# Two DRAM copies of the convolution's kernel rows, one for each half of the partitions

## What is computed

```python
def _L0_cond_ref(u, length, ...):          # B, H, L = 32, 64, 1024
    u_m = u * mask[:, None, :]
    kernel = _get_kernel(log_dt, C, log_A_real, A_imag, Lq)      # H x L
    y = irfft(rfft(u_m, n=2*Lq) * rfft(kernel, n=2*Lq))[..., :Lq]
    y = y + u_m * D[:, None]
    return y * mask[:, None, :]

def _L0_ffn_ref(x, ...):                   # hidden 1024, inner 2752
    gate, up = x2 @ Wg, x2 @ Wu            # weights unpacked from 4 bits
    return (gate * sigmoid(gate) * up) @ Wd

x = x + _L0_ffn_ref(_L0_cond_ref(x, ...))
```

## Time and profile before

| | us |
|---|---|
| median of 3 runs | 1163.69 (1163.19 to 1167.55) |
| profiled execution, its own time | 1166.86 |
| its span, first to last instruction | 1164.7 |
| mean granted TensorE clock | 0.993 |
| TensorE busy | 1141.1 (98%) |
| VectorE / ScalarE / GpSimd busy | 889.0 / 845.4 / 221.9 |
| 64 Toeplitz loads, issue to landing | 3.6 / 6.5 / 14.4 (min / median / max) |
| 9 kernel-row stores, issue to landing | 2.0 / 3.4 / 5.4 |

### The profile page before, as it was taken

How to read it: one execution, slowest core, us unless ns; L and a number is a source line. 1 busy time by engine, 2 the same in 40 slices (tenths; PEclk the granted TensorE clock), 3 DMA queues, 4 the chain that set the end, 5 groups by cost and what they waited for, 6 DMA issues and landing times.

```text
span 1164.7 us, 14987 instructions
## 1 busy us (share of the span) xinstructions
PE 1141.1 (98%) x5490; PEld 949.0 (81%) x5490; DVE 889.0 (76%) x987; ACT 845.4 (73%) x1402; POOL 221.9 (19%) x139
## 2 busy tenths in 40 slices
PE   5999999999999999999999999999999999999996
PEld 5999998788888888888888888888888888888884
DVE  7668746677777777777777887788788777777777
ACT  6443214888788788788788797887888788788773
POOL 0121000211422432121121251211211211211113
PEclk7999999999999999999999999999999999999999
DMA  7778779441553566434433874456655434434515
GB/s 275 274 230 254 251 246 255 113 109 27 151 149 100 135 161 166 121 87 109 117 100 101 237 210 125 106 154 193 160 154 141 122 101 117 109 88 121 129 39 212
DMA packets 76191, 176.03 MB, mean 151 GB/s; under 512 B 20870, under 2 KB 26438, under 8 KB 76118
## 3 DMA queue, kind: packets, MB, share of 16 engines
q1 hardware_dynamic: 74050, 173.24, 52.6%
q10 hardware_dynamic: 2036, 1.81, 0.5%
q0 software_dynamic: 32, 0.03, 0.0%
HBM read 159.94 MB, written 15.83 MB: 151 GB/s over the span
## 4 chain that ended last, share of the span: by engine, by line
PE 95%; DMA 1%; DVE 1%; issue 1%; POOL 0%; ACT 0%; DVEq 0%; POOLq 0%; SPq 0%
PE pair L1266 28%; PE pair L1307 27%; PE pair L1287 27%; PE pair L1219 12%; DMA toep<-kernel_padded 1%; POOL o L592 0%; DMA kernel_padded<-k_sb 0%; PE pair L1199 0%; PE pair L1177 0%; DMA logs<-in_L_cond_log_dt_dram 0%; DVE q_in L1061 0%; ACT size L644 0%; DVEq L165 0%; DVE exps L794 0%; ACT L646 0%
## 5 line engine op out<-in xcount | busy, mean ns | idle before, releaser
L1036 DVE SCALAR_TENSOR_TENSOR acc<-pair,s_down,acc 128x1024 f32<-128x1024 f32 x328 | 420.3, 1283 | 185.3 <-PE pair L1307 183.8
L711 ACT ACTIVATE pair<-pair,ratio 128x512 f32<-128x512 f32 x616 | 381.7, 664 | 99.5 <-PE pair L1266 99.2
L730 ACT ACTIVATE pair<-pair,ratio 128x512 f32<-128x512 f32 x581 | 360.2, 658 | 114.1 <-PE pair L1287 113.9
L1266 PE MATMUL pair<-high,wg 128*128 128x512 f32 x704 | 278.4, 395 | 0.0
L1266 PE MATMUL pair<-low,wg 128*128 128x512 f32 x704 | 276.1, 392 | 0.0
L1307 PE MATMUL pair<-mid_h,wd 128*128 128x512 f32 x688 | 268.7, 392 | 0.0
L1287 PE MATMUL pair<-high,wu 128*128 128x512 f32 x672 | 265.7, 395 | 0.0
L1307 PE MATMUL pair<-mid_l,wd 128*128 128x512 f32 x672 | 264.4, 393 | 0.0
L1287 PE MATMUL pair<-low,wu 128*128 128x512 f32 x672 | 263.4, 392 | 0.0
L544 POOL CAST mid_h<-sil 128x1024 fp32r<-128x1024 f32 (+1 forms) x43 | 45.3, 1052 | 688.3 <-DVE sil L1013 677.8
L1266 PEld LDWEIGHTS pair<-high,wg 128*128 128x128 f32 x704 | 132.1, 188 | 33.0 <-ACT pair L711 1.1
(11 more groups left out here) (154 smaller groups left out, 577.8 us busy)
## 6 DMA issues: line engine op xcount, KB each, us to landing
q_in<-rows_backwards SPq DMA_DIRECT2D x86, 512.0 KB, 4.7
z_in<-zeros_plus_one SPq DMA_DIRECT2D x130, 256.0 KB, 4.6
toep<-kernel_padded SPq DMA_DIRECT2D x64, 512.0 KB, 6.5
q_in<-_L_ffn_down_qweight_dram SPq DMA_DIRECT2D x42, 512.0 KB, 4.6
u_all<-in_x_dram SPq DMA_DIRECT2D x13, 512.0 KB, 10.7
x_fin<-in_x_dram SPq DMA_DIRECT2D x12, 512.0 KB, 9.0
out_dram<-x_fin SPq DMA_DIRECT2D x12, 512.0 KB, 5.2
high_parts<-staged SPq DMA_DIRECT2D x8, 512.0 KB, 3.0
```

The lines of the kernel that those rows point to most:

```text
L711: act.activation(gate_ps[:, tb, :], gate_ps[:, tb, :], ACT.Copy, scale=ratio[:, 0, G * t + g:G * t + g + 1]).then_inc(gate_scaled, 1)
L730: act.activation(up_ps(tau)[:, tb, :], up_ps(tau)[:, tb, :], ACT.Copy, scale=ratio[:, 1, G * t + g:G * t + g + 1]).then_inc(up_scaled, 1)
L1036: dve.scalar_tensor_tensor(out=acc[:, hid, :], in0=ps, scalar=scale, in1=acc[:, hid, :], op0=ALU.mult, op1=ALU.add).then_inc(down_taken, 1)
L1266: mm = pe.matmul(gate_ps[:, tb, :], w["g"][tau % 2][:, g, :], rows[:, g, 512 * tb:512 * tb + 512], start=g == 0 and part == 0, stop=part = ...
```

## The change

`kernel_padded` gets a second copy of all 64 rows. Every store of a chunk becomes two stores of the same `k_sb`, one to each copy; the zeros are written to both. Every Toeplitz load becomes two loads: partitions 0 to 63 read from copy 0, partitions 64 to 127 from copy 1, each 64 windows of 4 KB. The semaphores count 32 instead of 16 for a load, for a store and for the zeros.

```diff
--- before.py
+++ after.py
@@ -158,7 +158,7 @@
 
 def build_program(nc, x, itok, log_dt, C, log_A, A_imag, D, gq, gs, gz, uq, us, uz, dq, ds, dz,
                   ctab, stab, ident_in, out):
-    kpad = nc.dram_tensor("kernel_padded", (H, KPAD), F32, kind="Internal").ap()
+    kpad = nc.dram_tensor("kernel_padded", (2, H, KPAD), F32, kind="Internal").ap()
     rows_back = nc.dram_tensor("rows_backwards", (2 * TAIL + 1, 16, G, P), I32, kind="Internal").ap()
     high_back = nc.dram_tensor("high_parts", (KT, P, HALF), F32, kind="Internal").ap()
     zscr = nc.dram_tensor("zeros_plus_one", (3, ROWS, P), BF16, kind="Internal").ap()
@@ -361,23 +361,26 @@
             sp.dma_start(lens_i[:], bass.AP(itok.tensor, 0, [[0, P], [1, B]])).then_inc(lens_in, 16)
             for g in range(6, 14):
                 sp.dma_start(x_in(g), x_rows(g)).then_inc(x_loaded[g], 16)
-            sp.wait_ge(zero_stored, 16)
+            sp.wait_ge(zero_stored, 32)
 
             def store_kernels(c):
 
                 h0, n = CHUNKS[c]
                 sp.wait_ge(k_sb_ready, c + 1)
-                dst = bass.AP(kpad.tensor, h0 * KPAD, [[32, 32], [KPAD, n], [1, 32]])
-                sp.dma_start(dst, k_sb[:, 0:n, :]).then_inc(k_stored, 16)
-                sp.wait_ge(k_stored, 16 * (c + 1))
+                for copy in range(2):
+                    dst = bass.AP(kpad.tensor, (copy * H + h0) * KPAD, [[32, 32], [KPAD, n], [1, 32]])
+                    sp.dma_start(dst, k_sb[:, 0:n, :]).then_inc(k_stored, 16)
+                sp.wait_ge(k_stored, 32 * (c + 1))
 
             def load_toeplitz(g):
                 for hh in range(HG):
                     slot = HG * (g % 2) + hh
                     if g >= 2:
                         sp.wait_ge(conv_mm, (g - 2) * HG + hh + 1)
-                    src = bass.AP(kpad.tensor, (g * HG + hh) * KPAD, [[1, P], [1, L]])
-                    sp.dma_start(toep[:, slot, :], src).then_inc(t_loaded[slot], 16)
+                    for copy in range(2):
+                        p0 = P // 2 * copy
+                        src = bass.AP(kpad.tensor, (copy * H + g * HG + hh) * KPAD + p0, [[1, P // 2], [1, L]])
+                        sp.dma_start(toep[p0:p0 + P // 2, slot, :], src).then_inc(t_loaded[slot], 16)
 
             store_kernels(0)
             load_toeplitz(0)
@@ -521,7 +524,8 @@
             pool.memset(s_rows[:], 1.0).then_inc(rows_clear, 1)
             pool.memset(z_rows[:], 0).then_inc(rows_clear, 1)
             pool.wait_ge(const_ready, 1)
-            pool.dma_start(kpad[:, L:KPAD], zero[:]).then_inc(zero_stored, 16)
+            for copy in range(2):
+                pool.dma_start(kpad[copy, :, L:KPAD], zero[:]).then_inc(zero_stored, 16)
 
             pool.wait_ge(ai_loaded, 16)
             pool.wait_ge(c_loaded, 16)
@@ -914,7 +918,7 @@
                 h0, n = CHUNKS[c]
                 dve.wait_ge(k_mm, c + 1)
                 if c > 0:
-                    dve.wait_ge(k_stored, c * 16)
+                    dve.wait_ge(k_stored, c * 32)
                 do(dve.tensor_copy(k_sb[:, 0:n], k_ps[0:32, 0:32 * n].rearrange("p (h b) -> p h b", h=n)))
                 d_piece = bass.AP(d_row[:].tensor, h0, [[H, 32], [1, n], [1, 1]])
                 dve.tensor_tensor(k_sb[:, 0:n, 31:32], k_sb[:, 0:n, 31:32], d_piece, ALU.add).then_inc(k_sb_ready, 1)
@@ -1209,7 +1213,7 @@
                         multiply_kernel(chunk_begun_at(g - 2))
                     n = HG * g + hh
                     slot, k = n % TRING, hh // 2
-                    pe.wait_ge(t_loaded[slot], 16 * (n // TRING + 1))
+                    pe.wait_ge(t_loaded[slot], 32 * (n // TRING + 1))
                     if hh == 0:
                         pe.wait_ge(u_all_ready, 2 * HEAD_TURNS if g == 1 else 2 * g + 2)
                     if hh % 2 == 0 and g >= 2:
```

## The result

The changed kernel takes 1204.09 us in the median of 4 runs (1203.32 to 1210.85), the kernel before 1165.48 beside it: 1.034 times, 95% interval 1.032 to 1.037, 38.6 us slower. The forecast was 1181, 17 us slower. The measured time lies inside the range, 1170 to 1214, but where the rival "in between" (1190 to 1205) put it. The mechanism forecast is there, and it is less than half of the matter.

The account below looks back on a forecast made before the run. The prediction took TensorE, busy 98% of the span, to bound the kernel. Late loads at group 10 (13.3 us), at group 15 (1.7) and slower half loads (2.1) added 17.1 to 1163.7, giving 1181 us; range 1170 to 1214.

Parts of the forecast that it names:

- in between: Toeplitz loads: halves run at 205 to 250 GB/s, the DMA queue bounds now and then, 1190 to 1205 us; chance 0.16.
- The mechanism forecast: SP queue: added issues and second stores make Toeplitz loads late, so TensorE stalls; 13.3 us at group 10, 1.7 at group 15.
- Does half a load cost half?: SP queue: no; each added load issue costs 0.47 us, with 0.36 as the lower end.
- the 15.0 of the sum: SP queue, groups 2 to 9: added issues for 32 heads at 0.47 us each, 15.0 us.
- The queue's waits for others soak up 2.1: SP queue up to group 10's loads: its waits for others absorb 2.1 us, leaving those loads 15.6 us late.
- Rate of the half loads: DMA queue: half loads move at 250 GB/s, showing only behind the first weight loads, 2.1 us more for group 15's first head.
- The prediction's own sign: DMA, 60 to 120 us: share near 0.8 with 250 GB/s or more, or above 0.85 with about 200 or less for half rate.
- the halves also transfer at half rate: Toeplitz loads: halves go one behind the other, a head at about 205 GB/s; +50 us, 1213 us; chance 0.27.
- Not slower: Toeplitz loads: a second copy relieves a DRAM hot spot, giving back 6.6 us of store landings; 1166 us; chance 0.12.

Follow-up runs that it names:

- e2: The changed kernel with whole loads instead of cut ones, even heads from copy 0 and odd heads from copy 1, two stores per chunk: 1167.6 us.
- e7: The kernel before with its 64 weight transfers issued by ScalarE's queue instead of SP's: 1167.9 us.
- e9: Against the kernel before: two copies, one whole load per head, even partitions reading copy 0 and odd partitions copy 1: 1168.8 us.
- e4: The kernel before, one copy, with each head's load cut into even and odd partitions: 1180.8 us.
- e1: The kernel before, one copy and one store per chunk, with each head's load cut at partition 64: 1202.8 us.
- e5: The changed kernel with its 64 weight transfers issued by ScalarE's queue instead of SP's: 1193.5 us.
- e8: The kernel before, one copy, with partitions 0 to 63 loaded from SP's queue and 64 to 127 from GpSimd's: 1196.5 us.
- e10: The kernel before, one copy, with each head's load cut into three: partitions 32 to 95, 0 to 31 and 96 to 127: 1210.2 us.
- e3: The kernel before, one copy, with each head's load cut into two column halves over all 128 partitions: 1173.3 us.

## Why the prediction was wrong

**What bounds the kernel, what the change may win.** Right. The bound is TensorE; the convolution's losses go through nearly one for one (span +37.4, feed-forward stage +40.2 late and 2.8 shorter); nothing was to be won, which e2, e7 and e9 confirm from three sides.

**"Does half a load cost half? ... I take 0.47 us for each added issue."** The step that failed first. The direction was right and the row that told the truth was cited: L413, 64 partitions, at 636 ns against L417's 552. I used it only to exclude a cheaper half load and took the price of a whole one. Measured: 0.596 us an issue (4.96 us for eight), 0.79 us more per head, 32 x 0.79 = 25.3 us for the 15.0 of the sum. Scaling 0.431 by 636/552 would have given 0.50 an issue, still short.

**"The queue's waits for others soak up 2.1."** Right as far as it goes (after the change the queue waits 1.7 us for TensorE from 60 to 160 us and never for VectorE), but one more wait gives way: a store that is issued late into empty engines lands in 2 us instead of 4. In e4, with the same issues and fast halves, stores 3 to 6 hold the queue 6.9 us instead of 16.2, which takes 9 of the 25 us back: group 10's loads are issued 15.5 us late there, the forecast's 15.6, and the time is 1180.8, the forecast's own. That agreement is partly luck, an issue priced too low against a relief left out. One reading beside it is wrong, though the sum does not use it: the last eight weight transfers are issued behind group 10's loads, not before them (158.21 to 164.3 us in the changed kernel).

**"Rate of the half loads ... I take 250 GB/s ... so it shows only where the DMA queue is full."** The step that failed most. The rate itself was near: 200 to 280 GB/s. Wrong was that it hides. I compared the sum of the transfers (16.8 us) with the length of a round (25.4), as if the engines could work through all of it, but a store waits for what stands before it: stores 1, 2 and 3 held the queue 6.6 to 6.9 us and stores 7 and 8 7.0 to 7.6, against 2.4 to 5.4 before, and the loads behind them come late by the difference. Not all of that is the rate: with even and odd halves stores 1, 2 and 7 still held the queue 4.5, 4.7 and 6.1 us, but store 3 only 1.8 and store 8 3.0. e1 against e4 prices the slow rate at 7.8 us up to group 10 and 10.9 after it, 22 in the median; the sum had 2.1. The prediction's own sign pointed there: from 60 to 120 us the DMA engines moved 200 GB/s, what it named for the half rate (about 200 or less, the forecast 250 or more), at a share of 0.84, between its two values.

**The rival "the halves also transfer at half rate" (1213).** Its mechanism, halves cut at 64 that move slowly, is the one found, its size not: the kernel with relieved issues (e5) loses 26 us, not 50, as the rate falls to about 240 and not to 205, and part of the current loads run no faster to begin with. The Trainium skill's rule, in "SBUF — State Buffer", section "Door 1: The DMA port swizzle (why `[64,N]` ≈ `[32,N]`)", agrees in direction with e1 against e4 (257 against 401 GB/s), and the same page's section "Can I just issue two DMAs to hit both halves?" with e8. Where that last section calls one transfer over all 128 partitions the only way to reach all ports, e4 differs: transfers of 64 even or odd partitions ran at 401 GB/s, the rate of whole loads.

**The rival "in between" (1190 to 1205, chance 0.16).** It held in time and in rate: halves at 205 to 250 GB/s while the engines are busy (200/0.84 = 238 from 60 to 120 us), the DMA engines the bound now and then. What it did not say is where the loss arises: in the stores that wait behind half loads, and in the issues at 0.6 us.

**What nobody had on the list: the clock.** 8.8 us of longer TensorE work in the changed kernel, since most of its stalls are followed by matmuls at a lower granted clock. I priced stalls at their own length. It is in e1 and e10 too (0.94 and 0.89 from 130 to 190 us), twice in e4 and once in e3, where 48 matmuls behind 2.6 us of idling took 10.02 us; in e4 a stall of 2.5 us (at 53.8 us) was followed by the usual 7.09.

**"Not slower", by a hot spot in DRAM.** Refuted by e2 and e9: with two copies the median landing is 6.6 and 6.4 us against 6.5, and with the cut 6.1 (changed) against 5.9 (e1).

## What to carry to other kernels

Before a load is cut, ask three things of the trace: what one more issue costs with the new shape, whether the queue has slack for it, and whether the pieces still move at the full rate; a cut by even and odd partitions kept it here, a cut at partition 64 did not. Where a queue waits for a transfer to land, price the transfers in front of it as a wait and not as a sum against the length of the round. And a stall of TensorE can cost more than its length: of the changed kernel's stalls of 1.6 us or more behind 100 us, five cost 1.4 to 1.8 us on top and one nothing.

## What the runs showed of the hardware

- In runs of like loads an SP issue of 64 partitions takes longer than one of 128: 0.596 us (e1, e4 and the changed kernel) against 0.431 to 0.432 (before, e3), at 256 KB as at 512. In e10, pieces of 64, 32 and 32 partitions take 0.50, 0.58 and 0.42 us. Why is not shown.
- Later in a batch, with the engines full, halves cut at partition 64 move at 257 GB/s (e1), even/odd halves at 401 (e4), whole loads at 408 (before); two queues (e8) do not give the rate back.
- The first loads after an idle time run mostly at 150 to 300 GB/s with one copy, and when each load reads two (e9).
- After an idle time of 3.1 us the granted clock's mean was 0.66 over 5 us, after one of 2.7 us 0.59 over 4 us, and 48 matmuls took 1.6 to 1.7 us more; after 0.9 us of idling 64 matmuls took their usual 9.38, and after 2.99 us 48 took 7.12, nearly their usual time.
